# Transposes issued ahead of the scores in each slot of a fused deformable-gate and local-attention kernel

## The reference

```python
uk = jnp.concatenate([_unfold3(keyf, d) for d in (1, 2, 4)], axis=2)
uv = jnp.concatenate([_unfold3(value, d) for d in (1, 2, 4)], axis=2)
sim = jnp.sum(uk * query[:, :, None], axis=1, keepdims=True)
sim = jax.nn.softmax(sim, axis=2)
context = jnp.sum(sim * uv, axis=2)
return _conv1x1(context, w_w, w_b)
```

## Time and profile before

| | before |
|---|---|
| median of three executions | 1814.42 us (1812.4 to 1815.44) |
| the profiled execution's own time | 1815.19 us |
| its span, first to last instruction | 1813.5 us |
| TensorE matmul busy | 1659.0 us (91% of the span) |
| TensorE weight load busy | 1357.9 us (75%) |
| VectorE busy | 1377.1 us (76%) |
| ScalarE busy | 1025.4 us (57%) |
| GpSimd busy | 789.1 us (44%) |
| mean granted clock of TensorE | 0.981 of 2.4 GHz |

### The profile page before, as it was taken

The page is one execution under the profiler, slowest core; times in us unless marked ns, Lnnn a source line. Parts: engine busy times, 40 slices in busy tenths (PEclk is TensorE's granted clock), DMA queues, the critical chain, the costliest instruction groups (busy, mean ns, idle before and its releaser), DMA issues.

```text
span 1813.5 us, 36928 instructions
## 1 busy us (share of the span) xinstructions
PE 1659.0 (91%) x10439; PEld 1357.9 (75%) x10439; DVE 1377.1 (76%) x4742; ACT 1025.4 (57%) x2820; POOL 789.1 (44%) x1759
## 2 busy tenths in 40 slices
PE   1799999999999999999999999999999999999998
PEld 1477777778777777777777777777777777777776
DVE  5387877777877787877787877787877787877775
ACT  2256555555555556555555556555556555556564
POOL 4454443354443454443454543454543444543430
PEclk9999999999999999999999999999999999999999
DMA  3133443243443243443243443343443344433233
GB/s 112 29 94 119 133 134 100 71 124 119 133 127 96 73 133 119 133 122 93 80 133 119 133 121 90 84 133 119 133 121 85 88 131 121 133 120 89 51 100 111
DMA packets 73558, 197.68 MB, mean 109 GB/s; under 512 B 11536, under 2 KB 52880, under 8 KB 65168
## 3 DMA queue, kind: packets, MB, share of 16 engines
q1 hardware_dynamic: 73360, 195.32, 37.1%
HBM read 51.62 MB, written 51.38 MB: 57 GB/s over the span
## 4 chain that ended last, share of the span: by engine, by line
PE 57%; DVE 11%; issue 10%; POOL 9%; ACT 7%; DMA 3%; SPq 3%; ACTq 0%; DVEq 0%; POOLq 0%
PE ps_s L384 13%; PE ps_o L417 12%; PE ps_v L451 8%; PE ps_p L434 8%; PE ps_p L429 7%; PE ps_t L396 5%; POOL hats L693 4%; DMA ksp<-kk 3%; DVE e L894 2%; DVE stats L952 2%; ACT hats L599 2%; POOL hats L692 2%; SPq L334 2%; ACT qq L573 2%; ACT hid L589 1%
## 5 line engine op out<-in xcount | busy, mean ns | idle before, releaser
L547 ACT ACTIVATE e<-e,zmin 128x256 f32<-128x256 f32 x800 | 407.2, 509 | 682.3 <-DVE zmin L894 678.7
L417 PEld LDWEIGHTS ps_o<-eT,v 128*128 128x128 f32 x3584 | 498.7, 194 | 138.8 <-issue 134.6
L417 PE MATMUL ps_o<-eT,v 128*128 128x128 f32 (+1 forms) x3584 | 526.3, 274 | 2.0 <-ACT eT L562 1.7
L894 DVE CUSTOM_DVE_ANT_0 e<-ps_s,mask 128x256 f32<-128x256 f32 x800 | 334.0, 417 | 168.9 <-PE ps_s L384 148.2
L384 PE MATMUL ps_s<-kk,qq 128*128 128x256 f32 x1408 | 439.3, 394 | 0.0
L907 DVE TENSOR_SCALAR e<-e,rz 128x256 f32<-128x256 f32 x800 | 330.4, 413 | 0.0
L396 PE MATMUL ps_t<-ident,e 128*128 128x128 f32 x1600 | 309.4, 276 | 0.0
L451 PEld LDWEIGHTS ps_v<-wvox,xb 128*128 128x128 f32 x2048 | 259.0, 193 | 46.3 <-issue 43.2
L396 PEld LDWEIGHTS ps_t<-ident,e 128*128 128x128 f32 x1600 | 228.2, 143 | 83.2 <-issue 3.0
L451 PE MATMUL ps_v<-wvox,xb 128*128 128x128 f32 x2048 | 274.3, 277 | 5.5 <-issue 3.9
L936 DVE TENSOR_TENSOR v<-ps_v,bias 128x512 f32<-128x512 f32 x256 | 176.6, 690 | 118.3 <-PE ps_v L451 110.8
(11 more groups left out here) (154 smaller groups left out, 1727.0 us busy)
## 6 DMA issues: line engine op xcount, KB each, us to landing
raw<-in_x_dram SPq DMA_DIRECT2D x32, 1568.0 KB, 7.4
out_dram<-raw SPq DMA_DIRECT2D x32, 1568.0 KB, 5.4
v<-v SPq DMA_DIRECT2D x192, 256.0 KB, 3.8
kk<-kk SPq DMA_DIRECT2D x192, 112.0 KB, 2.2
ksp<-kk SPq DMA_DIRECT2D x192, 64.0 KB, 2.6
kk<-kk SPq DMA_DIRECT2D x32, 224.0 KB, 3.0
w_s<-in_w_dram SPq DMA_DIRECT2D x1, 64.0 KB, 6.4
wv_s<-in_wv_dram SPq DMA_DIRECT2D x1, 64.0 KB, 5.3
```

Of the source, the lines that this page charges most:

```text
L417: last = nc.tensor.matmul(o[:, UPIX * max(0, c - 1):UPIX * min(UNITS, c + 1)], v[:, s, c, :], eT[:, UPIX * (base + a):UPIX * (base + b)], ...
L547: nc.scalar.activation(e[:, i, :], e[:, i, :], ACT.Exp, bias=zmin[:, i:i + 1], scale=-1.0, accum_out=zs[:, i:i + 1]).then_inc(e_done.next( ...
L894: nc.vector.tensor_tensor_reduce(e[:, i, :], ps_s[(TILES * n.parity() + t) % 2][:, 0:KEYS], mask[:].rearrange("p s h a b -> p (s h a b)"), ...
```

## The change

In TensorE's `slot`, the call of `transposed` for the tile three slots old is put ahead of the call of `scores` for the new tile. Nothing else changes: the same instructions, waits, buffers and semaphores, in another order on one engine.

```diff
                     def slot(n, t):
                         if n.offset == first + 1:
                             tables(t)
-                        if n.exists():
-                            scores(n, t)
                         m, k = lagged(n, t, TRANSPOSE)
                         if m.exists():
                             transposed(m, k)
+                        if n.exists():
+                            scores(n, t)
                         for m, rel in items_at(n, t):
```

## The result

| | before | after |
|---|---|---|
| median, six executions each | 1815.5 us | 1824.7 us |
| lowest to highest | 1812.4 to 1818.95 | 1822.87 to 1826.01 |
| profiled execution, its span | 1813.5 us | 1822.9 us |
| mean granted clock of TensorE | 0.981 | 0.991 |

The ratio is 1.0044, with a 95% interval from 1.0031 to 1.0057. That is 5.2 us above the predicted 1819.5 and inside the range of 1810 to 1832.

A forecast was written before the change was run, and what follows sets the result against it. TensorE, busy 91% of the span, was the engine to follow. The 22 images keep 54.6 us, eight others add 4, the last 1.3: 1815.2 + 5.3 = 1820.5, less 0.8 for the profiled execution, given as 1819.5; range 1810 to 1832.

The forecast's parts named there:

- Scores later: Each way leaving TensorE at the scores gets 0.22 us of transposes ahead, regained only if it returns at the scores.
- ways 1 and 3: Slot 20 to 21 in all images, slot 2 to 3 in images without a clock fall: +0.22 us each.
- Way 2: Slot 9 to slots 11 and 15: both waits together +0.22 us each image, with L907 held by GpSimd.
- Way 4: Slot 5 to slot 10, leaving and returning at the scores: zero; the chain's wait at L481 also zero.
- Way 5: Last image: scores lead to a 0.33 us wait of L417 every second slot, six times, +1.3 us.
- Sum of an image: An image with a clock fall gets 0.44 us longer, one without 0.66.
- The clock takes part back: After the L481 wait: mean image stays 54.6 us, falls in about 0.4 of images instead of 15 of 22.
- The eight other images: Images with an L481 wait outside the 22: about 0.55 us longer each, at most 4.4, taken as 4.
- The clock gives nothing back: Rival: falls after the L481 wait come as often as before, 30 images cost 16.5 us, 1832 us; chance 0.25.
- Falls end: Rival: no falls after slot 1's L481 wait, the 22 images take 1192 us, total 1810; chance 0.12.
- It does nothing: Rival: the ways through the scores have hidden slack or another releaser, 1814.5 us; chance 0.13.

The follow-up runs named there:

- run 5: Kernel before with run 1's filling, transposes first in slot 20 alone: 1799.3 us, ratio 0.9902 to the kernel before, typical image +0.23 us over run 1.
- run 6: Kernel before with run 1's filling, transposes first in slot 2 alone: 1798.1 us, ratio 0.9905 to the kernel before, typical image +0.18 us over run 1.
- run 7: Kernel before with run 1's filling, transposes first in slot 9 alone: 1797.3 us, ratio 0.9896 to the kernel before, typical image +0.22 us over run 1.
- run 8: Kernel before with run 1's filling, transposes first in slot 12 alone: 1797.3 us, ratio 0.9899 to the kernel before, typical image +0.24 us over run 1.
- run 3: Kernel before with run 1's filling, transposes first in every slot but 2, 9, 12 and 20: 1797.6 us, ratio 0.9901 to the kernel before.
- run 2: Changed order in all slots, with run 1's filling: 1817.1 us, ratio 1.0016 to the kernel before, typical image 54.45 us.
- run 11: Changed order in all slots, with run 1's filling and a 16-column GpSimd memset ahead of the third bias block: 1820.3 us, ratio 1.0033 to the kernel before.
- run 12: Kernel before with transposes first in slots 12 and 20 alone, not filled: 1819.7 us against 1814.8, ratio 1.0024.
- run 1: Kernel before, its order kept, with six unread 128-column matmuls filling TensorE's wait at L481: 1792.5 us against 1814.2, ratio 0.9872.

## Why the prediction was right, and where it was short

**Scores later, ways 1 and 3: right.** Slot 20 was to cost 0.22 us in all images and costs 0.23 (run 5). Slot 2 was to cost 0.22 in those without a fall and costs 0.18 (run 6).

**Way 2: half right, mis-sized.** Slot 9 was to cost 0.22 and does (run 7). The step that failed is "GpSimd's work is shifted by one 0.22 only (it hangs on slot 9), so L907 ends one 0.22 later and not two". The hold of the earlier trace rows is real, but it does not stay in its place. (The wait for scores at 974.63 in the earlier trace rows is that of slot 12.) With VectorE another 0.2 us later, the L907 of the slot before falls behind GpSimd's L744, which it had beaten by 0.12 us (the rows of slot 12 above). Slot 12 alone costs 0.24 us (run 8). On the rule from "SBUF — State Buffer", section "Who interferes with whom", in the Trainium skill, that the later engine is blocked for the other's whole instruction: the later one is lengthened here as well, but not by that much. In run 8 GpSimd's step ends at 424.37 + 0.83 = 425.20 and L907 at 425.35, 0.15 later and not 0.35. Beside GpSimd's L693 it is not held for the whole instruction at all: in the rows of slots 20 to 1, before and after, L907 starts second and ends first. The prediction had named the price, 6.6 us for the program, should the hold not absorb the second wait; 0.24 us an image, 7.2 us, is about what was paid.

**Way 4: nearly zero, not zero.** The wait at L481 was to keep its length. From L429 in slot 21 to L481 an image takes 0.16 us more in run 3, where none of the four slots has changed, and 0.09 us an image is left net. In the timeline GpSimd's L693, ahead of L709, overlaps VectorE's L907 in another place: its first and third instruction take 0.83 and 0.77 us instead of 0.73 and 0.71, together the 0.16. They do so in the typical image of the changed kernel and of the runs 2, 3 and 11, where the slots other than 2, 9, 12 and 20 are exchanged, and in no other. That this is the cause was not tried by itself. Way 5, the last image: 1.3 us forecast, +1.8 in the end's stretch, which holds more than this way.

**Sum of an image.** 0.23 + 0.18 + 0.22 + 0.24 + 0.09 = 0.96 us against 0.66 forecast for one without a fall; measured 0.94 filled and 1.0 unfilled. Without slot 2 it is 0.78 for an image with a fall, against 0.44 forecast; measured about 0.74 (55.64 against 54.9).

**The clock takes part back: right in the mechanism, mis-sized in the count.** The mean granted clock rose from 0.981 to 0.991, and the mean image over the falls' stretch is held: 54.57, and 54.61 in run 12. By the medians the clock gives back 24.6 - 9.2 = 15.4 us, where the prediction had 17.8 - 5.3 = 12.5. But about 0.4 of the 22 images were to have a fall, and one had, since the images came out longer than the 54.2 and 55.3 forecast. With the measured sizes the working of the prediction gives (54.61 - 54.50) / (55.64 - 54.50) = 0.10 of the images with a fall, one in ten. In the trace, falls start at 301.83, 847.97 and 1557.94: ten and thirteen times 54.61 apart. Each image of 54.50 lies 0.11 us further back against that spacing, until a fall adds 1.1. For run 12 the same working gives (54.61 - 54.02) / (55.40 - 54.02) = 0.43, or ten of 23; there were seven, and three longer images without a fall. Why the falls keep to this spacing is open.

**The eight other images: mis-sized, and the size of the miss.** The prediction gave 4 us to the images outside the steady stretch. The five early ones alone took 9.0 longer. Before, they had one fall of their own (296.50) and took mostly 53.7 to 53.9 us. After, falls come at 134.58, 189.19, 264.29 and 301.83. Five images longer by 1.0 make 5.0, three more falls at 1.1 make 3.4, together 8.4. Why the falls start earlier is open; both programs also show a stretch at 0.50 around 80 us, before their steady part. One of these falls stands 19.7 us behind L481 (264.29 against 244.60), not after its wait, and the distances from it to its neighbours are no multiples of 54.61. The miss of 5.2 us is made up of 5.0 for the early images (9.0 against 4), 0.7 for the 25, 0.5 for the end, 2.1 less for the start, and 1.1 by which the kernel before was itself slower over six executions than over the three the prediction had. Two small slips in the prediction's sums change no argument: 1820.5 - 0.8 is 1819.7, and the gain where falls end is 3.7 instead of 3.9.

**The rivals.** "The clock gives nothing back", 1832, did not come in time, but its sum for what the ways cost (17.8) was too low: filled, it is 24.6. "Falls end" came true for nearly all of the steady stretch without the gain of 1810: with images of 54.50 instead of 54.2, 22 of them without a fall would take 1199 instead of 1201, so there was almost nothing to win. "It does nothing" is excluded by the result's interval and by run 2 against run 1.

## What to carry to other kernels

Before a step is put ahead of another on one engine, count the loops that leave that engine at the delayed step and come back elsewhere: here each of four cost about the whole delay in each image. A loop that seems covered by a hold between two other engines need not be, since the hold can move with the order in which they start. Where the clock falls at a wait, the falls can set the mean, and then the total time hides what an edit costs or saves; look at undisturbed images, or fill the wait in both versions. Filling that wait was itself worth 1.3% here, more than the order of the two steps.

## What was not expected of the hardware

- Six small matrix multiplies in a wait of about 1.8 us took the granted clock of the profiled execution from 0.981 to 0.999 and the median time from 1814.2 to 1792.5 us.
- With a shift of 0.17 us went one of 0.58: L907 took 0.35 us starting 0.12 us ahead of GpSimd's L744, and 0.93 starting 0.05 us behind it. GpSimd's step changed much less, from 0.92 to 0.83.
- To start first by the profile is not quite enough. In one image of run 1, L907 (here L920) starts 0.04 us ahead of L744 (here L757) and is held all the same:

```profile
1549.76 1.02 DVE L920 TENSOR_SCALAR e<-e,rz 128x256 f32<-128x256 f32 x1
1549.80 0.83 POOL L757 TENSOR_TENSOR btmp<-d_row,inside 128x384 f32<-128x384 f32 x1
```

- Nor does the order decide beside every step of GpSimd. L907 starts 0.12 us behind an L693 before, 0.34 behind it after, takes 0.39 and 0.35 us and ends first both times; it is L693 that takes 0.83 instead of 0.73. What sets L693 apart from L744 is open.
